# Three small moves in the order of TensorE's and VectorE's work in a four-block graph attention network

## The chip, the cores and the metric

The kernel runs on one core of one Trainium2 chip. The metric is the device time of one execution in microseconds (us). Five engines of the core work from queues of their own, each strictly in the order in which the program lists its instructions, and wait for each other on semaphores: TensorE (PE; its weight loads are listed apart as PEld), VectorE (DVE), ScalarE (ACT), GpSimd (POOL) and SyncE (SP, which here issues DMAs).

## The reference

Four graph layers in a row, each as `x = x + layer(relu(layernorm(x)))`, on 625 nodes with 512 features and 20,000 edges. The change touches the third layer alone, which is a chain of four attention blocks:

```
for i in range(NUM_BLOCKS):                      # 4 blocks
    y = _cond_layer_norm(x, cond, s1_w[i], s1_b[i], b1_w[i], b1_b[i])
    y = _sparse_attention(y, src, dst, wq[i], bq[i], wk[i], bk[i], wv[i], bv[i], wo[i], bo[i])
    x = x + y
    y = _cond_layer_norm(x, cond, s2_w[i], s2_b[i], b2_w[i], b2_b[i])
    y = jax.nn.relu(y @ m_w1[i] + m_b1[i]) @ m_w2[i] + m_b2[i]
    x = x + y
```

`_cond_layer_norm` is `(x - mean) * rsqrt(var + eps) * (1 + cond @ sw + sb) + cond @ bw + bb`. The attention has 4 heads of 128 features and ends in `out @ wo + bo`.

## The kernel before

The 625 nodes are five tiles of up to 128 rows (`NT` = 5; the last is `KEYS` = 116 wide). All operands of a product are kept as a high and a low part (`parts`), so that one product of 128 rows is three matmuls; a row tile of 512 outputs that sums over four slices of 128 features (`KT` = 4) is 12 matmuls. For every matrix that TensorE turns (transposes) or multiplies, ACT copies the high part out of PSUM and DVE then writes the low part as a difference.

PSUM holds three buffers of two banks (`big`) and two of one bank (`row`). They are used in a fixed rotation, given by the lists `BLOCK_BIG` and `BLOCK_ROW`: `free_big` and `free_row` make TensorE wait until the tile that used the buffer three, or two, uses ago was read (the counters `big_read`, `row_read`). DVE, ACT and POOL wait in turn for `big_full` and `row_full`.

The order of the work on each engine is written out by hand, in one function for each engine (`pe_l2`, `dve_l2`, `act_l2`, `pool_l2`), as straight code for the four blocks. Three stretches of a block matter here.

**The end of attention.** TensorE walks the list `ATT_PE` (L1974): scores `S` (L1842 by its products), turned probabilities `T` (L1872), and sums over the values, `PVa` and `PVb`, for the first 384 and the last 256 columns of nodes (L2006). DVE writes the low parts of a turned probability tile in L2384, and of a sum in L2392. The output product `@ wo` has one row tile for each node tile, `wo0` to `wo4` (all L1953). `row_begin` does its first 9 matmuls, over heads 0 to 2, and `out_end` the last 3, over head 3, after waiting for the low part of `PVa3` (tiles 0 to 2) or `PVb3` (tiles 3 and 4). DVE adds a finished row to the running `z` (`out_row`, L2289) and takes its statistics (`out_sums`, L2510; `out_moments`, L2514); POOL makes the reciprocal standard deviation from them.

**The second norm.** TensorE walks `SECOND_NORM`: `c1_t` is the conditional scale and bias of node tile t (L1896, two matmuls), `t1_t` turns the normalised tile (L1872, four). The rows `wo1` to `wo4` are put between them. Per tile, DVE does `centred` (L2259), `scaled` (L2268) and, after TensorE's turn and ACT's copy of the high part (L1565), `turned_rest` (L2274). The tiles `t1_3` and `t1_4` are turned late (`turn_late`, L2025), between the first products of the MLP. These are `hidden_sums` (L1848): for each of four slices `o` of the hidden layer a left half of 314 columns (nodes of tiles 0 to 2) and a right half, 12 matmuls each. The order is left half 0, `t1_3`, left half 1, `t1_4`, left half 2, then the right halves.

**The joint of two blocks.** The MLP's second product has rows `m2_0` to `m2_4` (L1953 again); DVE adds each to `z` (`hidden_row`, L2289 again) and takes its statistics. The first norm of the next block is begun in the same stretch: `c0_0` and `c0_1`, then `t0_0` between rows 3 and 4, `t0_1` after row 4, then `c0_2` and `c0_3`, which may overwrite the buffers of `c0_1` and of `t0_0`, and then the value product of tile 0 (`values`, L1923), whose four weight slices POOL has to finish (L1447) before they are used. There are three joints.

Of the kernel before, what the change touches and what calls it, by code (L numbers as in the profile page):

```python
# [19 lines left out]
NT = (N + P - 1) // P  # L20
# [170 lines left out]
def build(nc, a, out):  # L191
    ctx = ExitStack()
    with ctx:
# [1711 lines left out]
        def pe_l2(pe, turn_norm):  # L1905
# [6 lines left out]
            for it in range(BLOCKS):  # L1912
# [46 lines left out]
                def row_begin(name, t, left, w):  # L1959

                    free_row(pe, ROWBLK[f"{name}{t}"], nr)
                    row_terms(name, t, left, w, range(KT - 1))

                def out_end(t):


                    pe.wait_ge(big_read, BIGBLK["PVa3" if t < 3 else "PVb3"] + nb + 1)
                    row_terms("wo", t, qT, WO, range(KT - 1, KT)).then_inc(row_full, 1)
# [5 lines left out]
                for what, k, *tiles in ATT_PE:  # L1974

                    if (what, k) == ("PVa", HEADS - 1):
                        row_begin("wo", 0, qT, WO)
                    elif (what, k) == ("PVb", HEADS - 1):
                        out_end(0)
                        row_begin("wo", 1, qT, WO)  # L1980
                    if what == "k":
                        projected(what, k)
                        continue
                    name = f"{what}{k}"
                    if name not in ROW_SUMS:
                        u = BIGBLK[name]
                        free_big(pe, u, nb)
                    elif tiles[0][0] == 0:
                        free_row(pe, ROWBLK[name], nr)
                    if what == "S":  # L1990
                        h, t = k // NT, k % NT
                        pe.wait_ge(big_read, BIGBLK[f"k{h}"] + nb + 1)
                        wide_mm(pe, u, parts(nodes_of(qT, h, t), both(kT, h))).then_inc(big_full, 1)
                    elif what == "T":
                        pe.wait_ge(pn_up, it * HEADS * NT + k + 1)
                        turn(pe, u, pbuf[:, k % 4, :], NT).then_inc(big_full, 1)
                    else:
                        at = PV_COLS[what]
                        last = k * NT + at.stop // P - 1
                        pe.wait_ge(big_read, BIGBLK[f"T{last}"] + nb + 1)  # L2000
                        pe.wait_ge(vlo_up, (it + 1) * NT)
                        for st in tiles[0]:
                            terms = parts([vrow[0:KEYS[st], s, st, k * DH:(k + 1) * DH] for s in range(2)],
                                          [pT[0:KEYS[st], s, st, at] for s in range(2)])
                            for i, (l, r) in enumerate(terms):
                                ins = pe.matmul(head_sums(name, at.stop - at.start), l, r, start=(st == 0 and i == 0),  # L2006
                                                stop=(st == NT - 1 and i == len(terms) - 1))
                        if tiles[0][-1] == NT - 1:
                            ins.then_inc(row_full if name in ROW_SUMS else big_full, 1)
                rows = 1  # L2010
                for n in SECOND_NORM:

                    if n in ("c1_0", "c1_1", "c1_2", "t1_2"):
                        if rows > 1:
                            row_begin("wo", rows, qT, WO)
                        out_end(rows)
                        rows += 1
                    (cond if n[0] == "c" else turn_y)(1, int(n[3]), it)

                def turn_late(t):  # L2020
                    u = ROWBLK[f"t1_{t}"]
# [257 lines left out]
        def dve_l2(dve, tile_sums, tile_moments, tile_stats, entry_stats, f32, relu_rest, l3_norm, attention_mask):  # L2279
            norm_tile, centred, scaled, turned_rest = dve_first(dve, f32)  # L2280
            for it in range(BLOCKS):
# [114 lines left out]
                for t in range(NT):  # L2396
                    if t < NT - 2:
                        centred(1, t, it)
                    if t < NT - 1:
                        out_row(t + 1)  # L2400
                    if t == NT - 2:
                        turned_rest(1, t - 1, it)
                    if t >= NT - 2:
                        centred(1, t, it)
                    scaled(1, t, it)
                    if t < NT - 1:
                        out_sums(t + 1)
                    if 1 <= t < NT - 2:
                        turned_rest(1, t - 1, it)
                    if t < NT - 1:  # L2410
                        out_moments(t + 1)
# [24 lines left out]
                def hidden_row(t):  # L2436
                    residual("m2_", t, (it + 1) * 2 * NT + 1 + t)
# [20 lines left out]
                    continue  # L2458

                for t in range(NT):  # L2460
                    hidden_row(t)
                    if t == NT - 1:
                        turned_rest(0, 0, it + 1)
                    if 2 <= t < 4:
                        centred(0, t - 2, it + 1)
                    hidden_sums(t)
                    if 2 <= t < 4:
                        scaled(0, t - 2, it + 1)
                    tile_moments(*norm_tile(0, t, it + 1))
# [361 lines left out]
```

## Time and profile before

| | |
|---|---|
| median of 3 runs | 861.26 us (861.14, 861.26 and 864.45) |
| profiled execution, whole | 860.54 us |
| profiled execution, its span | 858.6 us |
| busy share of the span | PE 94%, PEld 82%, DVE 72%, POOL 56%, ACT 53% |
| busy of the 100 us from 300 us on | PE 98.3, DVE 60.8, ACT 54.5, POOL 57.2 us |
| the four blocks' output rows begin their last part at | 256.0, 400.0, 544.4 and 688.9 us |

The four blocks lie between about 150 and 740 us of the span and repeat every 144 us. In the rows below, times are counted in us from the span's start. Where several equal instructions stand in one row, "x12" is their number, the first time the first one's start and the second the time from there to the last one's end. A bracket gives the idle time of the engine just before and the instruction that ended it. The ends of matmuls are modelled by the profile, their starts are not.

### The profile page before, as it was taken

The page shows a single profiled execution, that of the slowest core. Times are in us where ns is not written, and L with a number is a line of the kernel's source. Part 1 is how long each engine was busy: PE and PEld are TensorE (multiplying, and loading weights), DVE is VectorE, ACT ScalarE, POOL GpSimd, SP SyncE. Part 2 cuts the span into 40 slices and gives each one's busy share as a digit, 9 for nine tenths or more (in the row PEclk, how much of TensorE's full clock was granted, in tenths as well). Part 3 has the DMA queues.
Part 4 walks back from the last instruction along what each step waited for, and adds up shares of the span by engine and source line. Part 5 has one row for each costly group of instructions (what it writes and reads, how often), then busy time and mean ns, then how long its engine had stood idle before and what let it go on. Part 6 is the DMA issues. An engine that isn't in the chain of part 4 may idle for free.

```text
span 858.6 us, 16355 instructions
## 1 busy us (share of the span) xinstructions
PE 804.9 (94%) x5978; PEld 706.0 (82%) x5978; DVE 620.8 (72%) x1272; ACT 451.7 (53%) x773; POOL 484.0 (56%) x542
## 2 busy tenths in 40 slices
PE   3988899999999999999999999999999999999896
PEld 2888677799998879898878999887999978875565
DVE  8999888955767664585775377677347776699996
ACT  5998572445751344673333367233447633256673
POOL 7344744686425579432666843367765339458871
PEclk9999999999999999999999999999999999999998
DMA  6000212332000243200033410014230002100211
GB/s 166 3 1 1 58 26 67 98 100 75 13 1 26 60 128 103 58 2 13 26 104 98 122 26 1 13 37 141 73 86 13 2 0 87 37 2 31 57 54 60
DMA packets 49762, 44.34 MB, mean 52 GB/s; under 512 B 6013, under 2 KB 37439, under 8 KB 49698
## 3 DMA queue, kind: packets, MB, share of 16 engines
q1 hardware_dynamic: 47234, 39.72, 16.2%
q10 hardware_dynamic: 2464, 3.80, 1.5%
q8 instruction: 37, 0.61, 0.3%
q14 instruction: 27, 0.22, 0.1%
HBM read 42.04 MB, written 1.33 MB: 51 GB/s over the span
## 4 chain that ended last, share of the span: by engine, by line
PE 70%; DVE 15%; ACT 5%; issue 4%; SPq 2%; POOL 2%; DMA 1%; DVEq 0%; POOLq 0%; ACTq 0%
PE psum L1842 20%; PE psum L1953 11%; PE psum L1848 10%; PE psum L2006 8%; PE psum L1872 6%; PE psum L1923 6%; PE psum L2145 3%; DVE arena L1029 2%; PE psum L951 2%; PE psum L1896 1%; PE psum L2147 1%; PE psum L893 1%; DVE stats L2510 1%; SPq L1265 1%; POOL ringw L1447 1%
## 5 line engine op out<-in xcount | busy, mean ns | idle before, releaser
L1376 POOL TENSOR_SCALAR acc<-acc,rden,flag 128x628 f32<-128x628 f32 x80 | 69.4, 867 | 105.4 <-DVE rden L2380 105.4
L1953 PE MATMUL psum<-ringw,arena 128*128 128x512 f32 (+1 forms) x480 | 119.4, 397 | 4.0 <-DVE arena L2392 2.5
L1842 PE MATMUL psum<-arena,ringw 128*128 128x314 f32 x768 | 114.2, 310 | 0.1
L1842 PEld LDWEIGHTS psum<-arena,ringw 128*128 128x128 f32 x768 | 112.8, 190 | 1.5 <-DVE arena L2357 1.1
L1953 PEld LDWEIGHTS psum<-ringw,arena 128*128 128x128 f32 (+1 forms) x480 | 86.8, 186 | 25.7 <-DVE arena L2392 3.5
L2384 DVE TENSOR_TENSOR arena<-psum,arena 128x640 fp32r<-128x640 f32 x80 | 65.7, 821 | 35.8 <-ACT arena L1634 35.8
L1842 PE MATMUL psum<-arena 128*128 128x314 f32 (+1 forms) x480 | 87.4, 320 | 2.5 <-DVE arena L2384 2.1
L2006 PE MATMUL psum<-arena 128*128 128x384 f32 (+3 forms) x480 | 82.4, 311 | 0.0
L1447 POOL TENSOR_TENSOR ringw<-raw,ringw 128x512 fp32r<-128x512 f32 x56 | 71.8, 1291 | 15.3 <-ACT ringw L1678 15.3
L2357 DVE SCALAR_TENSOR_TENSOR arena<-psum,cols,arena 128x628 fp32r<-128x628 f32 x32 | 27.9, 871 | 72.5 <-ACT arena L1616 72.5
L1872 PE MATMUL psum<-ident,acc 128*128 128x128 f32 (+1 forms) x528 | 76.3, 273 | 0.2
L1842 PEld LDWEIGHTS psum<-arena 128*128 128x128 f32 (+1 forms) x480 | 70.5, 187 | 6.5 <-DVE arena L2384 4.5
L2006 PEld LDWEIGHTS psum<-arena 128*128 128x128 f32 (+1 forms) x480 | 74.3, 189 | 0.6
L1447 POOL TENSOR_TENSOR ringw<-xn,ringw 128x512 fp32r<-128x512 f32 x49 | 65.3, 1338 | 16.7 <-ACT ringw L1678 16.7
L1634 ACT ACTIVATE arena<-psum 128x640 fp32r<-128x640 f32 x80 | 56.3, 703 | 33.8 <-PE psum L1872 32.3
L1629 ACT ACTIVATE acc<-acc,nsmax 128x628 f32<-128x628 f32 x80 | 65.1, 813 | 9.3 <-DVE nsmax L2375 8.9
L1872 PEld LDWEIGHTS psum<-ident,acc 128*128 128x128 f32 (+1 forms) x528 | 61.9, 139 | 8.0 <-DVE arena L2357 1.2
L2375 DVE CUSTOM_DVE_ANT_0 acc<-psum,mask 128x628 f32<-128x628 f32 x80 | 63.8, 801 | 0.2 <-issue 0.2
L1440 POOL TENSOR_SCALAR veps<-mv 128x1 f32<-128x1 f32 x60 | 13.7, 228 | 88.0 <-DVE mv L2514 86.0
L1565 ACT ACTIVATE arena<-psum 128x512 fp32r<-128x512 f32 x40 | 23.8, 594 | 74.8 <-PE psum L1872 59.4
L1848 PE MATMUL psum<-arena,ringw 128*128 128x314 f32 x384 | 58.4, 310 | 2.3 <-DVE arena L2274 2.3
L1923 PE MATMUL psum<-ringw,arena 128*128 128x512 f32 x240 | 58.9, 395 | 1.3 <-POOL ringw L1447 0.6
(321 smaller groups left out, 1830.5 us busy)
## 6 DMA issues: line engine op xcount, KB each, us to landing
raw<-in_L_gnn_m_w SPq DMA_DIRECT2D x16, 256.0 KB
xn<-in_L_gnn_m_w SPq DMA_DIRECT2D x16, 256.0 KB
raw<-in_L_gnn_wv SPq DMA_DIRECT2D x8, 256.0 KB
xn<-in_L_gnn_wv SPq DMA_DIRECT2D x8, 256.0 KB
raw<-in_L_gnn_wq SPq DMA_DIRECT2D x8, 256.0 KB
xn<-in_L_gnn_wq SPq DMA_DIRECT2D x8, 256.0 KB
raw<-in_L_gnn_wk SPq DMA_DIRECT2D x8, 256.0 KB
xn<-in_L_gnn_wk SPq DMA_DIRECT2D x8, 256.0 KB
```

The costliest lines, as they stand in the source:

```text
L1376: g.tensor_scalar(pbuf[:, k % 4, 0:NW], pbuf[:, k % 4, 0:NW], rden[:, k:k + 1], flag[:, 1, k % NT:k % NT + 1], ALU.mult, ALU.mult).then_in ...
L1447: g.tensor_tensor(to[1], place(n), to[0].bitcast(F32), ALU.subtract).then_inc(split_done, 1)
L1629: act.activation(pbuf[:, k % 4, 0:NW], pbuf[:, k % 4, 0:NW], ACT.Exp, bias=nsmax[:, k:k + 1], scale=-1.0, accum_out=den[:, k:k + 1]).then_ ...
L1634: act.activation(pT[:, 0, :, (k % NT) * P:(k % NT + 1) * P], bflat(u).rearrange("p (k n) -> p k n", k=NT), ACT.Copy).then_inc(phi_up, 1)
L1842: ins = pe.matmul(big[buf(u)][0:l.shape[1], h, 0:HW], l, r[:, h * HW:(h + 1) * HW], start=(i == 0), stop=(i == len(terms) - 1))
L1848: ins = pe.matmul(to, l, r, start=(i == 0), stop=(i == len(terms) - 1))
L1872: ins = pe.transpose(bflat(u)[0:KEYS[k], k * P:(k + 1) * P], src[:, k * P:k * P + KEYS[k]], ident[:, :])
L1923: ins = pe.matmul(brow(u), l, r, start=(k == 0 and i == 0), stop=(k == KT - 1 and i == 2))
L1953: ins = pe.matmul(brow(ROWBLK[f"{name}{t}"])[0:KEYS[t], :], l, r, start=(pieces[0] + i == 0), stop=(pieces[-1] == KT - 1 and i == len(term ...
L2006: ins = pe.matmul(head_sums(name, at.stop - at.start), l, r, start=(st == 0 and i == 0), stop=(st == NT - 1 and i == len(terms) - 1))
L2375: dve.tensor_tensor_reduce(wide(pbuf[:, k % 4, :]), bwide(u), wide(mask[:, t, :]), -DH ** -0.5, 3e38, ALU.add, ALU.min, nsmax[:, k:k + 1]) ...
L2384: dve.tensor_tensor(pT[:, 1, :, t * P:(t + 1) * P], bflat(u).rearrange("p (k n) -> p k n", k=NT), f32(pT[:, 0, :, t * P:(t + 1) * P]), ALU ...
```

## The change

Three moves; no instruction is added or taken away.

1. At the end of attention the nine first matmuls of `wo1` stand ahead of the three last of `wo0`, instead of behind them.
2. In the second norm, TensorE turns `t1_2` ahead of the three last matmuls of `wo4`, and DVE's `turned_rest` of that tile stands ahead of the `out_row` of tile 4.
3. At the joint DVE's `turned_rest` of `t0_0` stands ahead of the `hidden_row` of tile 4.

```diff
@@ PE, the end of attention
                     elif (what, k) == ("PVb", HEADS - 1):
+                        row_begin("wo", 1, qT, WO)
                         out_end(0)
-                        row_begin("wo", 1, qT, WO)
@@ PE, the second norm
                     if n in ("c1_0", "c1_1", "c1_2", "t1_2"):
                         if rows > 1:
                             row_begin("wo", rows, qT, WO)
-                        out_end(rows)
+                        if rows < NT - 1:
+                            out_end(rows)
                         rows += 1
                     (cond if n[0] == "c" else turn_y)(1, int(n[3]), it)
+                    if n == "t1_2":
+                        out_end(NT - 1)
@@ DVE, the second norm
+                    if t == NT - 2:
+                        turned_rest(1, t - 1, it)
                     if t < NT - 1:
                         out_row(t + 1)
-                    if t == NT - 2:
-                        turned_rest(1, t - 1, it)
@@ DVE, the joint
                 for t in range(NT):
-                    hidden_row(t)
                     if t == NT - 1:
                         turned_rest(0, 0, it + 1)
+                    hidden_row(t)
```

On TensorE at the end of attention, before: the last matmul that turns the last probability tile (L1872), the three matmuls that end `wo0` and wait for `big_read` (the low part of `PVa3`), the nine that begin `wo1` and wait for `row_read`, and `PVb3` (L2006).

```order
L1872 MATMUL psum<-ident,acc 116x128
L1953 MATMUL psum<-ringw,arena1 128x512 [waits split_done,big_read]
L1953 MATMUL psum<-ringw,arena1 128x512 x2
L1953 MATMUL psum<-ringw,arena1 128x512 [waits split_done,row_read]
L1953 MATMUL psum<-ringw,arena1 128x512 x8
L2006 MATMUL psum<-arena3,arena2 128x256 [waits vlo_up,big_read]
```

Now:

```order
L1872 MATMUL psum<-ident,acc 116x128
L1953 MATMUL psum<-ringw,arena1 128x512 [waits split_done,row_read]
L1953 MATMUL psum<-ringw,arena1 128x512 x8
L1953 MATMUL psum<-ringw,arena1 128x512 [waits split_done,big_read]
L1953 MATMUL psum<-ringw,arena1 128x512 x2
L2006 MATMUL psum<-arena3,arena2 128x256 [waits vlo_up,big_read]
```

The nine matmuls of `wo1` moved ahead of the wait for the low part of `PVa3`; the same stands in all four blocks.

On TensorE in the second norm, before: `wo4` (116 nodes), the turn of `t1_2`, then `c1_3` (L1896).

```order
L1953 MATMUL psum<-ringw,arena1 116x512 x8
L1953 MATMUL psum<-ringw,arena1 116x512 [waits split_done,big_read]
L1953 MATMUL psum<-ringw,arena1 116x512 x2
L1872 MATMUL psum<-ident,acc 128x128 [waits big_read]
L1872 MATMUL psum<-ident,acc 128x128 x3
L1896 MATMUL psum<-condw,condT 128x512 [waits big_read]
```

Now:

```order
L1953 MATMUL psum<-ringw,arena1 116x512 x8
L1872 MATMUL psum<-ident,acc 128x128 [waits big_read]
L1872 MATMUL psum<-ident,acc 128x128 x3
L1953 MATMUL psum<-ringw,arena1 116x512 [waits split_done,big_read]
L1953 MATMUL psum<-ringw,arena1 116x512 x2
L1896 MATMUL psum<-condw,condT 128x512 [waits big_read]
```

The turn moved ahead of three matmuls of 512 columns.

On DVE at the joint, before: the statistics of row 3 (L2514), then `hidden_row` of tile 4 (L2289), `turned_rest` of `t0_0` (L2274), the statistics of tile 4, and `centred` of tile 2 of the next block (L2259).

```order
L2514 BN_AGGR mv<-stats 128x2 [waits st_up]
L2289 TENSOR_TENSOR z<-psum,z 128x512 [waits xb_up,row_full]
L2274 TENSOR_TENSOR arena3<-psum,arena3 128x4x128 [waits yhi_up]
L2510 BN_STATS stats<-z 128x6 [waits row_read]
L2514 BN_AGGR mv<-stats 128x2 [waits st_up]
L2259 SCALAR_TENSOR_TENSOR acc<-z,mv,psum 128x512 [waits big_full,aggr_up]
```

Now (the lines after the change are numbered 3 higher here):

```order
L2517 BN_AGGR mv<-stats 128x2 [waits st_up]
L2277 TENSOR_TENSOR arena3<-psum,arena3 128x4x128 [waits yhi_up]
L2292 TENSOR_TENSOR z<-psum,z 128x512 [waits xb_up,row_full]
L2513 BN_STATS stats<-z 128x6 [waits row_read]
L2517 BN_AGGR mv<-stats 128x2 [waits st_up]
L2262 SCALAR_TENSOR_TENSOR acc<-z,mv,psum 128x512 [waits big_full,aggr_up]
```

The two instructions changed places, and with them the wait for ACT's copy (`yhi_up`) and the one for TensorE's row (`row_full`).

## Rows read from the trace of the kernel before

**Rows 1.** The page's first part: busy us, share of span, instructions of each engine.

```profile
PE 804.9 (94%) x5978; PEld 706.0 (82%) x5978; DVE 620.8 (72%) x1272; ACT 451.7 (53%) x773; POOL 484.0 (56%) x542
```

**Rows 2.** Waits of PE, 150 to 760 us: waiter, releaser, us, times, longest.

```profile
PE psum L1953 <- DVE arena L2392: 2.5, 4, 0.6
PE psum L1848 <- DVE arena L2274: 2.3, 4, 0.6
...
PE psum L1896 <- DVE arena L2274: 1.4, 3, 0.5
```

**Rows 3.** Timeline, end of attention in block 0: start, us, engine, instruction, idle before.

```profile
247.26 0.71 PE L1872 MATMUL psum<-ident,acc 128*128 128x128 f32 x5
...
247.73 0.96 PE L2006 MATMUL psum<-arena 128*128 128x256 f32 x6
...
250.88 0.41 DVE L2392 TENSOR_TENSOR arena<-psum,arena 128x256 fp32r<-128x256 f32 x1
...
254.68 0.71 PE L1872 MATMUL psum<-ident,acc 128*128 128x128 f32 x5
...
255.40 0.56 DVE L2392 TENSOR_TENSOR arena<-psum,arena 128x384 fp32r<-128x384 f32 x1 [3.39 <-ACT arena L1642]
...
256.02 3.01 PE L1953 MATMUL psum<-ringw,arena 128*128 128x512 f32 x12 [0.62 <-DVE arena L2392]
256.17 0.82 DVE L2384 TENSOR_TENSOR arena<-psum,arena 128x640 fp32r<-128x640 f32 x1 [0.21 <-ACT arena L1634]
...
261.28 0.42 DVE L2392 TENSOR_TENSOR arena<-psum,arena 128x256 fp32r<-128x256 f32 x1 [2.84 <-ACT arena L1642]
```

**Rows 4.** Timelines of DVE, PE and ACT, second norm of block 2.

```profile
558.58 0.74 DVE L2268 SCALAR_TENSOR_TENSOR acc<-acc,rstd,psum 128x512 f32<-128x512 f32 x1
...
560.52 0.66 DVE L2289 TENSOR_TENSOR z<-psum,z 128x512 f32<-128x512 f32 x1
561.52 0.69 DVE L2274 TENSOR_TENSOR arena<-psum,arena 128x512 fp32r<-128x512 f32 x1 [0.34 <-ACT arena L1565]
562.12 0.74 DVE L2259 SCALAR_TENSOR_TENSOR acc<-z,mv,psum 128x512 f32<-128x512 f32 x1
...
565.48 0.75 DVE L2268 SCALAR_TENSOR_TENSOR acc<-acc,rstd,psum 128x512 f32<-128x512 f32 x1
...
557.37 3.04 PE L1953 MATMUL psum<-ringw,arena 128*116 128x512 f32 x12
560.25 0.60 PE L1872 MATMUL psum<-ident,acc 128*128 128x128 f32 x4
...
562.36 1.97 PE L1848 MATMUL psum<-arena,ringw 128*128 128x314 f32 x12 [0.58 <-DVE arena L2274]
...
566.38 0.63 PE L2025 MATMUL psum<-ident,acc 128*128 128x128 f32 x4
...
560.89 0.60 ACT L1565 ACTIVATE arena<-psum 128x512 fp32r<-128x512 f32 x1 [2.64 <-PE psum L1872]
```

**Rows 5.** Timelines, joint of blocks 0 and 1; last row: joint of blocks 2 and 3.

```profile
297.66 1.07 PE L1896 MATMUL psum<-condw,condT 128*128 128x512 f32 x4
...
298.57 2.89 PE L1953 MATMUL psum<-ringw,arena 128*128 128x512 f32 x12
...
301.95 0.58 ACT L1565 ACTIVATE arena<-psum 128x512 fp32r<-128x512 f32 x1
...
304.01 0.17 DVE L2514 BATCH_NORM_AGGREGATE mv<-stats 128x2 f32<-128x6 f32 x1
...
304.88 0.71 PE L1896 MATMUL psum<-condw,condT 128*128 128x512 f32 x2
...
306.63 2.92 PE L1923 MATMUL psum<-ringw,arena 128*128 128x512 f32 x12
...
306.84 1.29 POOL L1447 TENSOR_TENSOR ringw<-xn,ringw 128x512 fp32r<-128x512 f32 x1
...
597.62 0.96 PE L1923 MATMUL psum<-ringw,arena 128*128 128x512 f32 x3 [0.38 <-POOL ringw L1447]
```

## The prediction

> **What bounds the kernel now.** I read the page's busy shares first. PE is busy for 94% of the span, DVE, the next of the computing engines, for 72% [rows 1]. In the blocks, which are where the change lies, PE hardly ever stops, so a block is as long as PE's work plus its few stops, and a change that moves work about without adding any can gain no more than those stops. The second view is the waits of PE over the four blocks [rows 2]. The largest sum is 2.5 us: four times, once in a block, the output product (L1953) waits for DVE's low part of `PVa3` (L2392). Next is 2.3 us: four times the first MLP product (L1848) waits for the low part of a turned tile (L2274). The third that the change touches is 1.4 us, in three joints, where `c0_3` (L1896) waits for the low part of `t0_0`. The three moves aim at these three, and the sum as this view counts it is 6.2 us. The third view is the timeline at each place, for what is late next.
>
> **How long a stop is.** The view counts PE's idle time from the modelled end of the matmul before. But in a running stream PE starts the next instruction well ahead of that end: five turns begin at 247.26, last 0.71 by the model, and the next matmul begins at 247.73, 0.47 after the first turn's start [rows 3]. So I price a stop from start to start. At the end of attention the five turns begin at 254.68, PE is ready at 254.68 + 0.47 = 255.15, and goes on at 256.02 [rows 3]: the stop is 0.87 us, where the idle column says 0.62. The Trainium skill bears on this: by "Perfetto Trace Analysis", section "Tensor Engine Instruction (MATMUL, LD_WEIGHTS)", a matmul's start is observed and its end is estimated from its size. By the idle column the first move below would be worth 2.5 us in all, by the starts 3.5; the trace agrees with the page, for its modelled end overlaps the next start wherever nothing is waited for.
>
> **Move 1, the end of attention.** Nothing is added. PE has nine matmuls of `wo1` to do where it now stops. They need row buffer 1, whose last tenant was read by DVE at 250.88 + 0.41 = 251.29 [rows 3], four us before, and weights and heads that `wo0` has just used. One matmul of this kind takes 3.01 / 12 = 0.25 us by the row, 0.24 from start to start, so the nine run from 255.15 to 257.3, and `out_end` of `wo0` then finds the low part of `PVa3`, finished at 255.40 + 0.56 = 255.96, waiting. It ends at about 258.0, and `PVb3` begins there, 0.87 earlier than before. It needs the low part of the last turned probabilities, finished at 256.17 + 0.82 = 256.99 [rows 3], so this is free too. What comes later than before is row 0's `out_row` and statistics on DVE: from 258.2, for some 1.4 us (0.66 for the row [rows 4], and I take as much for the statistics), to about 259.6. Behind them in DVE's queue stands the low part of `PVb3`, which was done at 261.28 and is now wanted at 260.4; 0.8 us are left. I take the whole stop: 4 x 0.87 = 3.5 us; the bounds are 2.5 (the idle column) and 3.5. No row of another kind enters, and a loss would need one of these three covers to be gone.
>
> **Move 2, the second norm.** Here the stop that is removed is not what sets the end. I use block 2's times as they stand; move 1 shifts all of them alike. `wo4` begins at 557.37, and its 12 matmuls are through at 560.25, when the turn begins, so nine are through at 559.53. The turn's input, `scaled` of tile 2, is ready at 558.58 + 0.74 = 559.32, just in time. ACT's copy began 0.64 after the turn before (560.25 to 560.89), now at 560.17, and lasts 0.60; DVE's `turned_rest` can start at 560.80 instead of 561.52 [rows 4]. It ends at 561.49, and the first MLP product follows 0.15 later (as 561.52 + 0.69 = 562.21 to 562.36), at 561.64, 0.72 earlier than 562.36 [rows 4]. So at that point PE is 0.7 us early. What is late next is the chain on DVE. It was free for `out_row` of tile 4 at 560.52; before, it did that and then idled 0.34 for ACT; now it idles from 560.52 to 560.80 and does both after that: 560.80, then 0.61 on (the distance from 561.52 to 562.12) `out_row` at 561.41, then `centred` of tile 3 at 562.01 to 562.07, against 562.12 before [rows 4]. DVE gains only 0.05 to 0.11 us. Its chain then goes on unchanged to `scaled` of tile 4, 565.48 + 0.75 = 566.23, and TensorE's late turn of that tile began at 566.38, 0.15 later [rows 4]: the same 0.15 with which it follows DVE when it is waiting for it. That turn was already set by DVE, though the idle column shows nothing there, and it stands in PE's queue ahead of the rest of the MLP. So PE's 0.7 us are given back as two new stops, at the late turns of tiles 3 and 4, and what remains is DVE's 0.1: 4 x 0.1 = 0.4 us. Bounds: 0, and the whole start-to-start stop, 4 x 0.7 = 2.9 us; I take the low value because the last pair of rows shows the chain with no slack.
>
> **Move 3, the joints.** `c0_2` begins at 304.88. Unhindered, four such matmuls and the next start take 298.57 - 297.66 = 0.91 us, so `values(0)` would begin at 304.88 + 0.91 = 305.79 instead of 306.63 [rows 5], 0.84 earlier. DVE is free for `turned_rest` at 304.01 + 0.17 = 304.18; ACT's copy of `t0_0` has been there since 301.95 + 0.58 = 302.53 [rows 5]; with 0.69 for the instruction [rows 4] it ends at 304.87, ahead of `c0_3`'s start. `hidden_row` of tile 4 is pushed from 304.72 to about 304.8, and the statistics behind it come earlier than before, since nothing stands between any more. What is late next is POOL: the fourth weight slice of `values(0)` is finished at 306.84 + 1.29 = 308.13. PE wants it at its tenth matmul, nine times 0.244 = 2.2 us after the start [rows 5]: before at 308.83, now at 307.99. So PE stops there until about 308.18, and the gain is 308.83 - 308.18 = 0.65 us. The second joint has the same distances. In the third PE already stops for POOL at the tenth matmul, until 597.62 [rows 5], so an earlier start there gains nothing. Sum: 0.65 + 0.65 + 0 = 1.3 us; bounds 0 and 3 x 0.84 = 2.5, the value between them by POOL's row. I take POOL's row as fixed, since move 3 touches nothing that POOL or the weights' DMAs wait for.
>
> **The sum.** 3.5 + 0.4 + 1.3 = 5.2 us. The profiled execution took 860.54 us whole, of it 858.6 span, so it would take 855.3. The median of the runs is 861.26, 0.7 above the profiled one; I forecast the median as 861.26 - 5.2 = 856.1 us. PE's shift is kept to the end, since what follows the blocks waits for their last rows.
>
> **Rivals.** *The stops are worth less than their starts say*: PE is held after the turns for some of the time that the model calls an end, or DVE's new place for row 0 delays `PVb3`, and POOL takes the joints' gain. Then 2.5 us from move 1, up to 0.4 and 0 to 1: 857.4 to 858.8. For it speaks that POOL has only 0.2 us between the two outcomes in a joint; against it the 0.47 in a plain row. *The late turns don't bind*: if DVE's chain ran on faster, or the late turn had slack that I don't see, move 2 gives its 0.7 in each block and the time is 856.1 - 2.5 = 853.6. Against it stands the 0.15. *Slower*: at the joint DVE's `turned_rest` now waits for ACT's copy with `hidden_row`, the statistics and the next `centred` queued behind it, and ACT's copy stands behind weight copies that wait for DMAs. In the first joint the copy is there 1.65 us before DVE is (302.53 against 304.18 [rows 5]), so this costs from a delay of 1.65 us on; the second I count alike, and the third, where POOL and the weights are later, from 0. With a delay d the loss is 2 x (d - 1.65) + d, against 3.9 us of moves 1 and 2: even at d = 2.4, and at d = 4 the time is 861.3 - 3.9 + 8.7 = 866.1. No row shows weights as late as that.
>
> **How the numbers follow.** The forecast as worked out, with its terms within some tenths, 0.62; the stops worth less, 0.26; the late turns not binding, 0.08; slower, 0.04. A measurement of this kernel tells about 0.5% from no change, 4.3 us: 856.95 is the border. The forecast and the second rival lie on the faster side, 0.70; the first rival is within, 0.26; slower 0.04. The range reaches from 854.2, part of the way to the second rival, to 858.6, nearly the whole of the first.
>
> **What would show each step.** Move 1: no wait of L1953 for L2392 in PE's waits, and about 0.9 us less from the last turns to `PVb3`. Move 2: the wait of L1848 for L2274 gone, and in its place waits of the late turns (L2025 before) for `scaled`, 0.2 to 0.4 us each, with the distance from `wo4` to the late turn of tile 4 about 0.1 shorter; if that is shortened by 0.7, I am wrong. Move 3: no wait of `c0_3`, and a stop of `values` for POOL in all three joints, about 0.2, 0.2 and 0.8 us. It would be wrong as a whole if PE's busy time grew.

## The result and the profile after

The changed kernel takes 857.4 us (median of 5 runs, 855.81 to 858.07), the kernel before 861.43 us beside it: a ratio of 0.9943 (95% interval 0.993 to 0.9957), 4.0 us less. The forecast was 856.1, the range 854.2 to 858.6. The profiled execution of the new kernel took 858.07 us, the longest of the five, with a span of 856.1.

The engines' busy times answer to [rows 1] and are the same within 2.1 us:

```profile
PE 807.0 (94%) x5978; PEld 707.6 (83%) x5978; DVE 620.7 (73%) x1272; ACT 452.2 (53%) x773; POOL 484.1 (57%) x542
```

PE's 2.1 us more is no growth: another execution of the same kernel (the whole change again, below) reads 804.4, against 804.9 before. The change only took out stops.

In the new kernel DVE's lines are numbered 3 higher (L2274 is L2277, L2392 is L2395, L2268 is L2271), and the late turn L2025 is L2028. The waits of PE, 150 to 760 us (waiter, releaser, us, times, longest), answer to [rows 2]:

```profile
PE psum L1842 <- DVE arena L2387: 2.2, 5, 0.5
PE psum L1923 <- POOL ringw L1447: 1.5, 2, 1.2
PE psum L1953 <- DVE arena L2428: 1.1, 1, 1.1
PE psum L2028 <- DVE acc L2271: 0.8, 3, 0.5
PE psum L1923 <- DVE arena L2277: 0.6, 1, 0.6
```

All three waits that the change aimed at, 6.2 us by this view, are gone. The waits of the late turns for `scaled` have grown from a single one of 0.2 us in the kernel before to three of 0.8 in all, and the wait of `values` (L1923) for POOL's weight slices from 0.6 to 1.5 us. The first, the third and the fifth row stand in the list of the kernel before with about the same sums.

**The end of attention.** PE and then DVE, block 0, answering to [rows 3] (all 1.85 us later in this execution, for reasons ahead of the changed code):

```profile
256.53 0.71 PE L1872 MATMUL psum<-ident,acc 128*128 128x128 f32 x5
257.00 3.01 PE L1953 MATMUL psum<-ringw,arena 128*128 128x512 f32 x12
259.84 1.36 PE L2006 MATMUL psum<-arena 128*128 128x256 f32 x10
...
257.25 0.56 DVE L2395 TENSOR_TENSOR arena<-psum,arena 128x384 fp32r<-128x384 f32 x1 [3.38 <-ACT arena L1642]
...
260.04 0.69 DVE L2292 TENSOR_TENSOR z<-psum,z 128x512 f32<-128x512 f32 x1 [1.20 <-PE psum L1953]
...
262.25 0.42 DVE L2395 TENSOR_TENSOR arena<-psum,arena 128x256 fp32r<-128x256 f32 x1 [0.79 <-ACT arena L1642]
```

The matmuls of the output rows now begin 0.47 after the turns, as in a plain row of [rows 3], and the sum's low part (257.25) is made under them. Row 0 comes to DVE later, at 260.04, but DVE still has 0.79 us to spare ahead of the next low part.

**The second norm.** PE, DVE and ACT, block 0, answering to [rows 4]:

```profile
269.99 2.34 PE L1953 MATMUL psum<-ringw,arena 128*116 128x512 f32 x9
272.17 0.60 PE L1872 MATMUL psum<-ident,acc 128*128 128x128 f32 x4
272.52 0.93 PE L1953 MATMUL psum<-ringw,arena 128*116 128x512 f32 x3
...
274.27 1.97 PE L1848 MATMUL psum<-arena,ringw 128*128 128x314 f32 x12
276.38 0.63 PE L2028 MATMUL psum<-ident,acc 128*128 128x128 f32 x4
...
278.89 0.63 PE L2028 MATMUL psum<-ident,acc 128*128 128x128 f32 x4 [0.16 <-DVE acc L2271]
...
273.44 0.69 DVE L2277 TENSOR_TENSOR arena<-psum,arena 128x512 fp32r<-128x512 f32 x1 [0.17 <-ACT arena L1565]
274.05 0.68 DVE L2292 TENSOR_TENSOR z<-psum,z 128x512 f32<-128x512 f32 x1
274.64 0.74 DVE L2262 SCALAR_TENSOR_TENSOR acc<-z,mv,psum 128x512 f32<-128x512 f32 x1
...
278.00 0.75 DVE L2271 SCALAR_TENSOR_TENSOR acc<-acc,rstd,psum 128x512 f32<-128x512 f32 x1
...
272.81 0.60 ACT L1565 ACTIVATE arena<-psum 128x512 fp32r<-128x512 f32 x1 [1.93 <-PE psum L1872]
```

The first product (274.27) no longer stops, but `scaled` of tile 4 ends at 278.75 and the late turn follows it 0.14 later.

**The joints.** First joint (PE, its weight loads, POOL), answering to [rows 5], then PE in the third joint:

```profile
305.80 1.17 PE L1896 MATMUL psum<-condw,condT 128*128 128x512 f32 x4
306.81 3.27 PE L1923 MATMUL psum<-ringw,arena 128*128 128x512 f32 x12
309.92 0.60 PE L1872 MATMUL psum<-ident,acc 128*128 128x128 f32 x4
...
309.12 0.53 PEld L1923 LDWEIGHTS psum<-ringw,arena 128*128 128x128 f32 x3 [0.52 <-POOL ringw L1447]
...
307.25 0.55 POOL L1442 TENSOR_TENSOR rstd<-veps,half 128x1 f32<-128x1 f32 x1
307.77 1.29 POOL L1447 TENSOR_TENSOR ringw<-xn,ringw 128x512 fp32r<-128x512 f32 x1
...
591.34 1.52 PE L1896 MATMUL psum<-condw,condT 128*128 128x512 f32 x4
592.69 2.42 PE L1923 MATMUL psum<-ringw,arena 128*128 128x512 f32 x9
596.30 0.96 PE L1923 MATMUL psum<-ringw,arena 128*128 128x512 f32 x3 [1.18 <-POOL ringw L1447]
597.10 0.60 PE L1872 MATMUL psum<-ident,acc 128*128 128x128 f32 x4
```

In the first joint `c0_3` no longer stops, but the tenth value matmul does: POOL's slice ends at 309.06 and its weights are loaded at 309.12. PE's own row hides that stop among its twelve matmuls (3.27 instead of 2.92 us); the row of the weight loads shows it. In the third joint the stop grew from 0.38 [rows 5] to 1.18 us.

The whole time of an execution varies by some 2 us with what lies ahead of the blocks (the last turns of block 0 began at 254.68 in the profile before and at 256.53 here). So below, each part is measured as the distance between the starts of two PE instructions, in us (from times printed to 0.01), for the blocks 0 to 3 or the joints 1 to 3:

| kernel | last turns to `PVb3` | late turn 3 to late turn 4 | `PVb3` to late turn 4 | `c0_2` to the turn of `t0_2` | last turns of block 0 to late turn 4 of block 3 |
|---|---|---|---|---|---|
| before | 4.19 4.18 4.19 4.19 | 2.21 2.56 2.21 2.21 | 19.13 19.51 19.16 19.13 | 4.50 4.50 5.13 | 456.20 |
| after | 3.31 3.31 3.31 3.31 | 2.51 2.87 2.51 2.51 | 19.05 19.40 19.05 19.05 | 4.12 4.14 5.76 | 452.18 |

The blocks became 4.02 us shorter: 4 x 0.88 = 3.5 from the first move, 0.08 + 0.11 + 0.11 + 0.08 = 0.38 from the second, and 0.38 + 0.36 - 0.63 = 0.11 at the three joints, where the third move lies. The 0.63 lost in the third joint is not shown to be that move's doing; the single moves below speak against it.

### The profile page after: what moved, and what is told of

It is laid out like the page before. It is cut to its first block, busy times and chain, and to the rows that moved or that the text cites. A ratio compares the mean times of both kernels' runs of the same rounds, so it can differ in the third digit from the quotient of the medians.

```text
span 856.1 us, 16355 instructions
## 1 busy us (share of the span) xinstructions
PE 807.0 (94%) x5978; PEld 707.6 (83%) x5978; DVE 620.7 (73%) x1272; ACT 452.2 (53%) x773; POOL 484.1 (57%) x542
## 4 chain that ended last, share of the span: by engine, by line
PE 65%; DVE 16%; issue 5%; POOL 4%; ACT 4%; DMA 3%; SPq 3%; DVEq 0%; POOLq 0%
PE psum L1842 20%; PE psum L2006 8%; PE psum L1953 8%; PE psum L1848 8%; PE psum L1872 6%; PE psum L1923 5%; PE psum L2148 3%; POOL ringw L1447 2%; DVE arena L1029 2%; SPq L1265 2%; PE psum L1896 1%; DVE stats L2513 1%; PE psum L2150 1%; PE psum L893 1%; PE psum L951 1%
## 5 line engine op out<-in xcount | busy, mean ns | idle before, releaser
L2006 PE MATMUL psum<-arena 128*128 128x384 f32 (+3 forms) x480 | 82.4, 311 | 0.0
L1872 PE MATMUL psum<-ident,acc 128*128 128x128 f32 (+1 forms) x528 | 76.3, 273 | 0.2
L2006 PEld LDWEIGHTS psum<-arena 128*128 128x128 f32 (+1 forms) x480 | 74.3, 189 | 0.6
L1872 PEld LDWEIGHTS psum<-ident,acc 128*128 128x128 f32 (+1 forms) x528 | 61.7, 139 | 8.2 <-DVE acc L2271 1.5
L1440 POOL TENSOR_SCALAR veps<-mv 128x1 f32<-128x1 f32 x60 | 13.7, 228 | 87.2 <-DVE mv L2517 85.3
L1923 PE MATMUL psum<-ringw,arena 128*128 128x512 f32 x240 | 59.6, 397 | 2.3 <-POOL ringw L1447 1.5
```

What stands on the lines that cost most here:

```text
L1872: ins = pe.transpose(bflat(u)[0:KEYS[k], k * P:(k + 1) * P], src[:, k * P:k * P + KEYS[k]], ident[:, :])
L1923: ins = pe.matmul(brow(u), l, r, start=(k == 0 and i == 0), stop=(k == KT - 1 and i == 2))
```

## The experiments

Twelve runs follow, one of them the changed kernel again; a ratio is to the kernel before, run beside each. Among the versions of the changed kernel most of the intervals overlap, so what tells them apart are the distances in their traces.

| kernel | median us | ratio (95%) |
|---|---|---|
| first move alone | 858.04 | 0.994 (0.9921 to 0.9959) |
| second move alone | 861.12 | 0.9987 (0.9972 to 1.0001) |
| third move alone | 861.74 | 0.9986 (0.997 to 1.0002) |
| the whole change again, beside these | 857.55 | 0.9934 (0.9914 to 0.9955) |
| after + POOL's slice first | 855.98 | 0.9928 (0.9915 to 0.9941) |
| after + DVE's `centred` first | 856.49 | 0.9936 (0.9924 to 0.9949) |
| after, short statistics of tile 4 | 855.15 | 0.9917 (0.9902 to 0.9932) |
| before, short statistics of tile 4 | 861.63 | one run |
| after + both orders | 855.16 | 0.9911 (0.9897 to 0.9925) |
| after + 24 more waits in SP's program | 856.27 | 0.9935 (0.9919 to 0.9952) |
| after + both orders + these waits | 855.04 | 0.9909 (0.9892 to 0.9926) |
| after + 150 waits in TensorE's program | 857.75 | 0.9941 (0.9921 to 0.9961) |

**The first move alone.**

```diff
-                        out_end(0)
                         row_begin("wo", 1, qT, WO)
+                        out_end(0)
```

> Move 1 alone, on the kernel before. My theory: the stop at the end of attention is as long as its starts say, 0.87 us, and all of it is kept, so the run is 3.5 us shorter than before (ratio about 0.996), and the distance from the last turns of attention to PVb3 falls from 4.19 to 3.31 us in all four blocks. Rival, the idle column is right: 2.5 us shorter, distance 3.57 us.

Measured: last turns to `PVb3` 3.29, 3.30, 3.28 and 3.31 us, and the late turns as in the kernel before. So 0.88 to 0.91 us went from each block: the start-to-start price of 0.87 us is right and the idle column's 0.62 too small. This move carries most of the gain (3.14 of the some 4 us over the blocks).

**The second move alone.** The edit is the second and the third hunk of the change:

```diff
-                        out_end(rows)
+                        if rows < NT - 1:
+                            out_end(rows)
...
+                    if n == "t1_2":
+                        out_end(NT - 1)
...
-                    if t < NT - 1:
-                        out_row(t + 1)
                     if t == NT - 2:
                         turned_rest(1, t - 1, it)
+                    if t < NT - 1:
+                        out_row(t + 1)
```

> Move 2 alone. My theory: DVE's chain sets TensorE's late turn of tile 4, so only 0.1 us per block is gained, 0.4 us in all (ratio 0.999 to 1.000); the wait of the first MLP product for L2274 is gone and waits of the two late turns for DVE's scaled stand in its place. Rival, the late turns do not bind: 0.7 us per block, 2.9 us in all (ratio 0.9967).

Measured: `PVb3` to late turn 4 19.04, 19.37, 19.05 and 19.03, so about 0.4 us shorter in all; the late turns 2.52, 2.86, 2.52 and 2.52 apart, as in the whole change. The 2.9 us of the stops that it removed are not to be had this way. The ratio alone could not tell 0.4 us from nothing.

**The third move alone.**

```diff
-                    hidden_row(t)
                     if t == NT - 1:
                         turned_rest(0, 0, it + 1)
+                    hidden_row(t)
```

> Move 3 alone. My theory as corrected by the trace of the changed kernel: POOL's fourth weight slice sets values(0), so 0.4 us is gained in each of the first two joints and nothing in the third, 0.8 us in all, less where the third joint's weights come late (ratio 0.999). The distance from c0_2 to the turn of t0_2 is 4.1 us in the first two joints (4.50 before) and 5.1 us or more in the third. Rival, as in the prediction: 0.65 us in two joints. Rival, POOL does not bind: 0.8 us in each of three, 2.5 us.

Measured: 4.08, 4.14 and 5.29 us from `c0_2` to the turn of `t0_2`: 0.42 and 0.36 gained, 0.16 lost in the third joint. The ratio leaves open whether that is a gain.

**The whole change, again.** The same kernel as after, beside the three.

> All three moves, beside the single ones on one chip. My theory: the gains add, since the places lie apart: 3.5 + 0.4 + 0.8 = 4.7 us (ratio 0.9945). Rival, they share a limit: clearly less than the sum of the three single runs.

Measured: 451.96 us over the blocks, 4.24 less than before, with 4.12, 4.10 and 5.59 in the joints. The three moves alone took 3.14, 0.30 and 0.49 from the blocks (453.06, 455.90 and 455.71 against 456.20), 3.93 together. So the parts add up within 0.3 us. The third joint differs from kernel to kernel by more than that: with the first move alone, which does not touch it, it took 5.67 instead of 5.13, and with the second alone 5.10.

**POOL's fourth slice first.** POOL makes a reciprocal (L1440, L1442) between the third and the fourth slice; here the slice goes first.

```diff
-                    rests(WV, 0, 3)
+                    rests(WV, 0, KT)
                     rstd_of(LN_BLK + it * 2 * NT + 3, NT + 3)
-                    rests(WV, 3, KT)
```

> The changed kernel, and on POOL the fourth value weight slice is finished ahead of the reciprocal deviation of tile 3 instead of behind it (both instructions of 0.19 and 0.55 us). If POOL's order is what took the joint's gain, the stop of values(0) for POOL goes from the first two joints and shrinks by about 0.8 us in the third: 0.4 + 0.4 + 0.8 = 1.6 us shorter than the changed kernel. Rival, the weights' DMAs and ACT set the slice: nothing changes. Rival, the later deviation of tile 3 holds up scaled and the turn of t0_3: up to 0.8 us per joint lost.

Measured: 3.74, 3.75 and 4.68 us. PE and POOL in the first joint:

```profile
304.30 1.17 PE L1895 MATMUL psum<-condw,condT 128*128 128x512 f32 x4
305.31 2.90 PE L1922 MATMUL psum<-ringw,arena 128*128 128x512 f32 x12
308.04 0.60 PE L1871 MATMUL psum<-ident,acc 128*128 128x128 f32 x4
...
304.09 2.54 POOL L1446 TENSOR_TENSOR ringw<-xn,ringw 128x512 fp32r<-128x512 f32 x2
306.71 0.19 POOL L1439 TENSOR_SCALAR veps<-mv 128x1 f32<-128x1 f32 x1
```

The fourth slice ends at 306.63, ahead of its matmul, and PE runs through. So POOL's order is what took half of the third move's gain in the first two joints.

**DVE's `centred` first.** In the second norm `centred` of tile 3 goes ahead of `out_row` of tile 4 (tile 4 itself has no `out_row` behind it, so nothing changes there).

```diff
-                    if t < NT - 1:
-                        out_row(t + 1)
                     if t >= NT - 2:
                         centred(1, t, it)
+                    if t < NT - 1:
+                        out_row(t + 1)
```

> The changed kernel, and on DVE centred of tile 3 in the second norm stands ahead of out_row of tile 4 instead of behind it, so that scaled no longer follows directly on the instruction whose result it reads. If DVE's chain sets the late turns, both come 0.15 to 0.2 us earlier in each block, 0.6 to 0.8 us shorter in all than the changed kernel. Rival, the late turns do not bind: no difference.

Measured: `PVb3` to late turn 4 18.87, 19.22, 18.85 and 18.87, 0.18 to 0.20 less than after. The late turns follow DVE's chain.

**Short statistics of tile 4, after.** The statistics of tile 4 in the second norm are taken over 64 of the 512 columns, so the output is another one.

```diff
-                    tile_sums(norm_tile(1, t, it)[1], z[:, t, :])
+                    tile_sums(norm_tile(1, t, it)[1], z[:, t, 0:64] if t == NT - 1 else z[:, t, :])
```

> The changed kernel, with the statistics of tile 4 in the second norm taken over the first 64 of 512 columns (this changes what is computed), which takes some 0.5 us out of DVE's chain between the two late turns. If that chain binds, the distance between the late turns falls from 2.51 us to about 2.16, what TensorE's own work needs: 4 x 0.35 = 1.4 us shorter than the changed kernel. Rival, it does not bind: no difference.

Measured: late turns 2.21, 2.40, 2.20 and 2.20 apart, and no wait of L2028 in the list. In blocks 0, 2 and 3 the late turn of tile 4 begins 0.30 us after `scaled` ends, so 2.20 is TensorE's own distance there. In block 1 it still begins 0.15 after: there DVE sets it even now, though the list of waits has no row for it. The third joint took 6.63 us in this run, which hides part of the gain in the median.

**Short statistics of tile 4, before.** The same edit, in the kernel before.

> The kernel before with the second norm's statistics of tile 4 taken over 64 of 512 columns, which takes some 0.5 us out of DVE's chain ahead of scaled of tile 4; the output is another one. Theory: in the kernel before, the late turn of tile 4 is reached by DVE's chain and by TensorE at the same time (2.21 us from the late turn of tile 3, which the run with the same cut in the kernel after showed to be TensorE's own distance). Then the distance stays at 2.21 in blocks 0, 2 and 3, and falls from 2.56 to 2.2 to 2.4 in block 1; the whole is at most 0.4 us shorter. Rival: DVE alone sets it, as the prediction says: the distance falls to about 1.9 in every block, and the whole is 1.2 us or more shorter.

Measured: 2.17, 2.18, 2.17 and 2.17, against 2.21, 2.56, 2.21 and 2.21. DVE and then PE, block 2, answering to [rows 4]:

```profile
565.86 0.75 DVE L2268 SCALAR_TENSOR_TENSOR acc<-acc,rstd,psum 128x512 f32<-128x512 f32 x1
...
567.19 0.60 PE L2025 MATMUL psum<-ident,acc 128*128 128x128 f32 x4
```

`scaled` now ends at 566.61, 0.58 us ahead of the late turn instead of 0.15, and the turn comes hardly earlier: in blocks 0, 2 and 3 shortening DVE's chain by half a microsecond gave 0.04 us. There DVE and TensorE reached the late turn together; only in block 1 did DVE set it alone.

**Both orders.** The edits of POOL and of `centred` in one kernel.

> The changed kernel with both reorderings, POOL's fourth slice ahead of the deviation and DVE's centred of tile 3 ahead of out_row of tile 4. The two places lie apart, so the gains add: 1.6 + 0.7 = 2.3 us shorter than the changed kernel, ratio to the kernel before about 0.992.

Measured: 855.16 us, 3.76, 3.74 and 4.60 in the joints, 18.85 to 18.89 (19.21 in block 1) to the late turn; 449.62 us over the blocks, 2.56 less than after and 2.34 less than in the whole change again. By the ratios alone the step is less clear: 0.9911 lies under 0.9943 and 0.9934, but its interval overlaps that of the second of these.

**24 more waits in SP's program.** The remaining question was the third joint. SP issues the weights of a joint one after the other, and one issue stands out. SP's durations of one issue on line L1265, min/median/max in ns, and that issue, in the kernel after:

```profile
L1265 SPq DMA_DIRECT2D raw<-in_L_gnn_b_w x16: 320/420/449, 123.1 to 576.9; - x16
L1265 SPq DMA_DIRECT2D xn<-in_L_gnn_s_w x16: 385/420/1442, 126.3 to 580.9; - x16
...
579.41 1.44 SPq L1265 DMA_DIRECT2D xn<-in_L_gnn_s_w  x1
```

```diff
-            sp.wait_ge(const0, 3)
+            for i in range(25):
+                sp.wait_ge(const0, 3)
```

The 25 waits replace one, so 24 are added, where the expectation counts 25.

> The kernel after with 25 more waits in SP's program, each already fulfilled, ahead of the loop over the blocks, where SP stands idle anyway. In the kernel after, one single issue of SP, the third copy of the third conditional weight of block 3, takes 1.44 us where the others take 0.42, and all later weights of the third joint stand behind it. Theory: the long issue belongs to a place in SP's program (the instruction after it comes late), so 25 more instructions ahead of it put it 25 instructions earlier, into the loads of block 2, where nothing waits for it. Then no issue of that line is longer than 0.5 us, the weights of the third joint come about 1 us earlier, the distance from c0_2 to the turn of t0_2 falls there from 5.5 to 4.3 to 4.8 us, and the time is 0.7 to 1.1 us under that of the kernel after. Rival: it belongs to what else the chip does at that moment (transfers, the queue's fill); then the same issue stays at 1.2 to 1.7 us, the distance at 5.4 to 5.8, and the time is that of the kernel after.

Measured: the same issue takes 1.84 us, and the third joint 5.64 (the rows give 5.76 for the kernel after, not the 5.5 of the expectation). The theory fell: 24 instructions more in SP's program did not move the long issue.

**Both orders and these waits.**

> The version with both further moves (POOL's fourth weight slice ahead of a reciprocal, DVE's late centred tiles ahead of the output row) and the 25 waits as well. If the long issue of SP moves away, the third joint's 4.60 us from c0_2 to the turn of t0_2 become 3.75 to 4.1, and the time is 0.5 to 0.9 us under 855.2, about 854.5; if it stays, 855.2.

Measured: 855.04 us, the same as without the waits; the long issue is there (1.47 us), the third joint 4.19 (4.60 without them). The median gained nothing that the measurement can tell.

**150 waits in TensorE's program.** In the time of the long issue the DMA view of the kernel after, from 579.2 to 581.2 us, shows a packet that carries instructions (queue, packets, MB, share); it lies at 579.6:

```profile
q8 instruction: 1, 0.02, 2.9%
```

There is none on that queue in SP's weight stretches of the first two joints, where no issue is long. In all 13 traces other than that of the run below, the packet lies within 0.3 us of the start of the long issue (before: 581.1 and 581.35).

```diff
+            for i in range(150):
+                pe.wait_ge(const0, 1)
             pe.wait_ge(const0, 3)
```

> The kernel after with 150 more waits, each already fulfilled, at the start of TensorE's program, where TensorE stands idle for its first 9 us. Extra waits in SP's program did not move the long issue of the third joint. In its time (579.41 to 580.85) the trace shows one packet on queue q8, which carries instructions (at 579.6; in the kernel before at 581.1, in the run with more waits on SP at 577.2); in the first two joints these packets lie at 282.0 and 306.5, 423.5 and 445.5, outside SP's stretches of weight issues there (286.6 to 298.8, 429.6 to 441.8). Theory: these packets are TensorE's program, and an issue of SP that meets one is held for about 1 us. 150 more instructions ahead put the packets about 9 to 15 us earlier: to about 571 and 591, 292 and 433. Then the third joint has no issue longer than 0.5 us and its distance from c0_2 to the turn of t0_2 falls from 5.5 to 4.1 to 4.4 us, while in the first and second joint one issue becomes 0.7 to 1.6 us long and the distance there grows from 4.1 to 4.4 to 5.5. Rival: the place has nothing to do with the packets; then the third issue of the third joint stays at 1.2 us or more, the distances at 4.1, 4.1 and 5.5. The time itself may carry up to 3 us for the waits at the start.

Measured: packets of that queue now lie at 294.8, 432.6 and 572.0 us, and the long issues have moved with them. Line L1265, and the long issues of the first and the second joint:

```profile
L1265 SPq DMA_DIRECT2D raw<-in_L_gnn_s_w x16: 326/420/881, 118.6 to 573.9; - x16
L1265 SPq DMA_DIRECT2D raw<-in_L_gnn_b_w x16: 319/420/1592, 121.6 to 577.3; - x16
L1265 SPq DMA_DIRECT2D xn<-in_L_gnn_s_w x16: 386/420/445, 124.8 to 580.3; - x16
L1265 SPq DMA_DIRECT2D xn<-in_L_gnn_b_w x16: 419/420/1597, 127.8 to 583.4; - x16
...
294.61 1.60 SPq L1265 DMA_DIRECT2D xn<-in_L_gnn_b_w  x1
...
432.46 1.59 SPq L1265 DMA_DIRECT2D raw<-in_L_gnn_b_w  x1
```

From `c0_2` to the turn of `t0_2` it takes 5.30, 5.47 and 4.80 us: 1.2 and 1.3 more than after in the first two joints, 0.96 less in the third. The third fell less than expected because its packet still met the first weight of the stretch (0.88 us). So a load of TensorE's instructions that met one of these weight issues of SP cost a joint about a microsecond, and which joint it was depended on how many instructions TensorE had behind it. The length of the issue does not give the length of the joint by itself: 2.0 us went with 6.63 (short statistics, after), but 1.84 with 5.64 and 1.44 with 5.76.

## Why the prediction held, and where it did not

**What bounds, and how long a stop is: right.** PE's busy time did not grow (804.9 us before, 807.0 and 804.4 in two executions after), and the only gains were its stops. The first move gave 0.88 us a block, where start to start said 0.87 and the idle column 0.62.

**Move 1: right.** 3.5 us forecast, 3.5 measured. Of the three covers, the last held by the margin that was given: 0.8 us forecast, 0.79 idle in DVE's row.

**Move 2: right in size, and nearly in mechanism.** The first product came 0.68 us earlier after `PVb3` (15.11 to 14.43; 0.72 forecast), and 0.30 was lost again at each of the two late turns (0.2 to 0.4 forecast), so 0.08 to 0.11 stayed. One sentence was too strong: "That turn was already set by DVE". The run with short statistics in the kernel before shows that in three of four blocks TensorE arrived there at the same moment. A chain that ends 0.15 us ahead of its reader need not be the only one that ends there. The result was the same, since TensorE's part came 0.7 earlier and DVE's only 0.1. The rival of unbound late turns, 853.6, has fallen.

**Move 3: the term that was mis-sized.** 0.65 + 0.65 + 0 = 1.3 us forecast, 0.38 + 0.36 - 0.63 = 0.11 measured at the three joints; that is 1.2 us, nearly all of the 1.3 between 856.1 and 857.4. POOL was named as what is late next, and its slice did stay fixed: it ended 3.25 us after `c0_2` began before (308.13 - 304.88 [rows 5]) and 3.26 after (309.06 - 305.80). But the old time of the tenth matmul was worked out with 0.244 us a matmul, which has a modelled end in it. A narrow window of PE's timeline in the kernel before would have shown its start:

```profile
308.69 0.85 PE L1923 MATMUL psum<-ringw,arena 128*128 128x512 f32 x3
309.38 0.60 PE L1872 MATMUL psum<-ident,acc 128*128 128x128 f32 x4
```

The same three matmuls in the kernel after:

```profile
309.12 0.96 PE L1923 MATMUL psum<-ringw,arena 128*128 128x512 f32 x3
```

Before, the tenth began at 308.69, not 308.83: 0.14 of the 0.65. The mistake that the second paragraph of the prediction warns of went into its own third move. The other 0.13 is for the most part the restart: from the start of the tenth matmul to the next turn it takes 0.80 us (309.12 to 309.92), where it took 0.69 before (308.69 to 309.38); the eleventh begins 0.34 after the tenth, where a running stream has 0.23. The 0.84 us that the joint would give without POOL was a little high too: with POOL's slice first it gave 4.50 - 3.74 = 0.76, because `c0_2` and `c0_3` unhindered take 1.01 us from start to start here (305.80 to 306.81), not the 0.91 of [rows 5].

The third joint was forecast at 0 because POOL bound it already, and "I take POOL's row as fixed". It was not: POOL's fourth slice came 0.62 us later, counted from late turn 4 of block 2 (596.30 - 564.44 = 31.86 against 597.62 - 566.38 = 31.24). That can't be laid to move 3 alone: by the same count the slice came 0.15 later with move 3 alone, but 0.50 later with move 1 alone and 0.47 later in the kernel before with short statistics, and neither of these has move 3. The place moves with what else shifts in time, and the prediction had no term for that. The long issue of SP was there before the change too (1.21 us; 1.44 after; 1.16 to 2.0 in the other eleven kernels that met it there). It accounts for some 0.23 of the 0.62: SP's first value issue starts 0.24 later by the same count (585.66 - 564.44 against 587.36 - 566.38). The rest appears between the issue of the value slices and their arrival at ACT, where another 256 KB load, issued by ACT (L1590), runs at the same time; no run took that apart, and it stays open.

**The rivals.** The first, stops worth less, is right for the joints and wrong for move 1. By the time alone it could not be told from the forecast: 857.4 is the lower edge of its band, and 1.3 above the forecast. What speaks for the forecast is the distances: move 1 gave 3.5, where the rival had 2.5. *Slower* needed ACT's copy at the joint to be late, behind weight copies that wait for DMAs. In the first two joints DVE waits for nothing there. In the third it does, as the timelines of DVE and ACT show:

```profile
591.38 0.69 DVE L2277 TENSOR_TENSOR arena<-psum,arena 128x512 fp32r<-128x512 f32 x1 [0.75 <-ACT arena L1565]
...
589.60 1.26 ACT L1678 ACTIVATE ringw<-raw 128x512 fp32r<-128x512 f32 x2 [2.03 <-DMA raw<-in_L_gnn_wv]
590.77 0.58 ACT L1565 ACTIVATE arena<-psum 128x512 fp32r<-128x512 f32 x1
```

ACT waited 2.03 us for the first value slice, and its copy of `t0_0` stood behind that. `c0_2` and `c0_3` take 1.52 us there instead of 1.17, but POOL's slice is later than that, so these 0.35 us are covered. The mechanism was there, a good deal below its price.

**The whole.** 4.02 us over the blocks against 5.2 forecast, and 4.0 between the medians. The prediction put 0.70 on times under its border of 856.95; 857.4 lies above it, so on that side the chances missed, by the joints' 1.2 us.

## What to carry to other kernels

Price a stop of TensorE from the start of what runs ahead of it to the start of what follows, and use start-to-start times for every matmul of the sum, also for the one that decides when the next resource is needed. Where one stop is removed, look at the next two engines that the same stretch waits for: here DVE's chain took back 0.6 of 0.7 us in each block, POOL half of a joint's gain, and only putting their queues in the new order as well (855.16 us) brought more. Where parts are smaller than the spread of whole executions, the distances between starts inside the trace tell them apart when medians don't.

## What the runs showed of the hardware that was not expected

**Loads of instructions disturb DMA issues.** The view of the queues lists packets of kind "instruction" on q8, 37 in the execution. In 13 traces the weight issue of SP that met such a packet in the third joint took 1.2 to 2.0 us instead of 0.42; 150 waits more in TensorE's program moved packets and long issues together, 24 more in SP's did not move them. Of all 3119 issues of SP between 100 and 800 us in the 14 traces, 38 are over 0.3 us longer than the median of their line, and every one of the 38 overlaps a packet of kind "instruction", 28 of them one on q8 and the other 10 one on a second queue, q14. The reverse does not hold: 87 issues that overlapped a packet on q8 were not longer in this sense. In four runs a value weight of the third joint met a packet on q14 and took 0.77 to 1.05 us instead of 0.37. What sets apart the issues that are held up, no run shows.

**Ends of matmuls.** The Trainium skill's "Perfetto Trace Analysis", section "Tensor Engine Instruction (MATMUL, LD_WEIGHTS)", says that a matmul's end is estimated. The traces agree, and show how much it hides: a stop of 0.87 us read as 0.62, and the stop at the tenth value matmul of the first joint is not seen in PE's merged row. By starts it is 0.25 us (0.48 from the ninth to the tenth, where a running stream has 0.23), and with the 0.11 of the restart 0.36; putting POOL's slice first gave back 0.38. The row of the weight loads shows the stop too, but as 0.52, which is too much.
